# A graph layer with routed experts: 125-row transfers cut into 112 and 13 rows, and a rebuilt expert stage

## The chip, the cores and the metric

The kernel runs on one core of one Trainium2 chip. The core has five engines that run beside one another, each with its own instruction queue: PE (TensorE, matrix products), DVE (VectorE), ACT (ScalarE), POOL (GpSimd) and SP (SyncE, which here only issues transfers). Transfers between the chip's memory and the on-chip buffers run on 16 DMA engines. The metric is device time in microseconds (us) of one launch; less is better.

## The reference

The input is 1250 nodes of 768 values, and 41,250 directed edges. One layer is computed:

```python
xn = layernorm(x)
x  = x + gnn(xn, edges) + mix(xn)        # gnn: two graph-attention layers, 4 heads of 512, then 1 of 768
x  = x + ffn(layernorm(x))               # mix: random-feature attention of 8 heads, linear in the nodes

# ffn: two-level routing, 2 of 4 groups and 2 of 8 experts in each, so 4 of 32 experts for a node
comb = combine_weights(xf)               # [1250, 32], four entries of a row are not zero
h = gelu(einsum('nd,edm->nem', xf, W1) + b1)     # W1 [32, 768, 384]
y = einsum('nem,emd->ned', h, W2) + b2           # W2 [32, 384, 768]
out = einsum('ne,ned->nd', comb, y)
```

## The kernel before

**Tiling.** The 1250 nodes are 10 tiles (NT) of 125 rows (P); rows lie on the partitions of the on-chip buffers. All arithmetic is float32 but for selection matrices in bfloat16. There is no scheduler: each stage writes one instruction list per engine by hand, with semaphores between them, and a barrier of all engines ends a stage.

**Stages.** In order of time: norm (layernorm of x, 0 to 60 us), mix in two halves (60 to 485), proj (its output product and the first residual x1, 485 to 615), count (edges are turned into a dense matrix of edge counts, 615 to 938), mask (counts turned, masks and row maxima, 938 to 1053), gat1 (first attention layer, head by head, 1053 to 1470), gat2p and gat2 (second layer, 1470 to 1903), route norm (1903 to 1968), route (logits to expert choices, 1968 to 2033), expert (2033 to 2648).

**Transfers.** SP issues almost all of them, in program order, and waits in its queue hold back what is behind. Where a tensor is cut into tiles of 125 rows its transfer has 125 rows on the chip's side too: the loads of x in two halves (L131), x for the residual (L314), the count rows of a mask tile (L907), the 50 loads of a count tile for attention (L1048), x1 and the masks together (L1260, L1261), and the stores of x1, of the normed rows and of the output. Vectors needed on all rows are spread over 125 partitions by `partition_broadcast(P)`.

**Route.** POOL makes constants, DVE picks the experts, PE counts and ranks the nodes of each expert. DVE then makes `posm` (rank of a node within each expert, -1 where it isn't chosen), `ntile` (turns of 128 nodes per expert) and `tstart` (first turn of each).

**Expert stage.** Work goes by turns: one turn is up to 128 nodes of one expert, and there are 52 turns here. For each turn DVE compares rank minus offset with a row of 0 to 127 (Q, L1928), PE multiplies Q with `codes` (10 short products, PI, L1995) and thereby finds which nodes they are and their gates; DVE makes indices of them (L1887 to L1895), POOL gathers the rows (X) by an indirect transfer, PE turns X (TX, L2006), DVE and ACT copy it to xT, PE multiplies it with W1 (PH, 6 products of 384 columns with xT held still, L2034), DVE adds the bias, ACT takes gelu, PE turns h (TH, L2013), ACT copies hT, PE multiplies with W2 (PY, L2023), DVE and ACT scale by the gate into y, and POOL adds y into the output by an indirect transfer (L1850). It is a pipeline over four turns: while turn n is looked up, n-1 is in the first product and n-2 in the second. Four experts' weights are held at a time (NB = 4); SP loads the next ones as slots come free, and issues the first four at the end of the route norm's list. A stage's closing barrier stands in the trace under the line of the stage's `with ExitStack()`: L1456 for route norm, L1590 for route.

## Time and profile before

| | |
|---|---|
| median of 3 runs | 2640.47 us (2627.52 to 2644.08) |
| profiled execution, span | 2648.0 us (its own device time is not given beside it; the span is 7.5 us over the median) |
| PE busy | 2149.9 us, 81% |
| DVE busy | 1172.5 us, 44% |
| ACT busy | 443.9 us, 17% |
| POOL busy | 190.2 us, 7% |
| hardware transfer queue q1 | 82727 packets, 210.86 MB |
| mean transfer rate | 105 GB/s |

The span is the time from the first to the last instruction of the profiled execution. "Busy" is the time in which an engine had an instruction under way, so what is missing to the span is waiting. An average over 11 stages with different limits says little; the rows further down are taken stage by stage. "PEclk" is the clock granted to PE as a share of 2.4 GHz: 1.0 is full speed and 0.5 is 1.2 GHz. "DMA share" is how much of the 16 DMA engines' time was taken.

### The profile page before, as it was taken

To read this page: it belongs to the slowest core of one execution; us is meant where nothing else is said; L and a number is where in the kernel's file an instruction comes from. 1 tells how busy PE (TensorE), PEld (TensorE's weight loads), DVE (VectorE), ACT (ScalarE), POOL (GpSimd) and SP (SyncE) were. 2 spreads that over 40 slices of the span, in tenths; PEclk is the share of its full clock that TensorE was granted. 3 is DMA by queue.
4 is the path that set the end of the run, shared out by engine and by line. 5 is a ranking of instruction groups with operands and counts; after the bars stand their busy time and mean duration, and the time that the engine had idled before them with its cause. 6 is when DMAs were issued, how large, how long until landed. Compare 5 with 4: busy or idle time off the path is not lost. (4 is left out here: it accounts for less than half of the span.)

```text
span 2648.0 us, 32969 instructions
## 1 busy us (share of the span) xinstructions
PE 2149.9 (81%) x8696; PEld 1415.3 (53%) x8697; DVE 1172.5 (44%) x2660; ACT 443.9 (17%) x721; POOL 190.2 (7%) x205
## 2 busy tenths in 40 slices
PE   2998998596999922599999799539846888988997
PEld 1666665452555512488888455215543555555554
DVE  3113213133666626579888011056434444444442
ACT  1232112100111112122222000000000222222221
POOL 0000000000000000000000000000001222222222
PEclk9998998897999955799999899769956999989999
DMA  4001200113000045222322411321152777778653
GB/s 162 40 0 63 81 0 36 70 44 117 23 23 24 22 150 184 112 111 95 115 99 81 161 62 55 130 80 48 31 206 81 207 210 225 219 240 257 163 122 66
DMA packets 104535, 278.90 MB, mean 105 GB/s; under 512 B 8053, under 2 KB 53159, under 8 KB 103067
## 3 DMA queue, kind: packets, MB, share of 16 engines
q1 hardware_dynamic: 82727, 210.86, 22.6%
q0 software_dynamic: 15184, 55.37, 9.1%
q10 hardware_dynamic: 6560, 11.86, 1.2%
q8 instruction: 37, 0.61, 0.1%
q14 instruction: 27, 0.21, 0.0%
HBM read 214.49 MB, written 63.57 MB: 105 GB/s over the span
## 5 line engine op out<-in xcount | busy, mean ns | idle before, releaser
L1179 PE MATMUL gat_Z<-h,gat_wt 125*125 125x256 f32 (+1 forms) x1600 | 356.4, 382 | 40.0 <-DVE gat_wt L1095 40.0
L1179 PEld LDWEIGHTS gat_Z<-h,gat_wt 125*125 125x125 f32 x1600 | 299.3, 189 | 85.7 <-DVE gat_wt L1095 40.5
L2034 PE MATMUL ex_PH<-ex_w,ex_xT 128*128 x636 | 240.3, 532 | 24.2 <-DVE ex_xT L1883 14.5
L542 PE MATMUL mix_G<-mix_w,mix_xs 128*125 128x384 f32 x720 | 243.4, 489 | 0.0
L2023 PE MATMUL ex_PY<-ex_w,ex_hT 128*128 (+1 forms) x660 | 223.7, 489 | 15.9 <-POOL ex_hT L1838 14.8
L825 PE MATMUL count_G<-gnn_w,xnT 128*125 (+1 forms) x480 | 214.3, 596 | 18.5 <-issue 18.5
L1329 PE MATMUL gat2p_Y<-gat2p_w,gat2p_hT 128*125 128x384 f32 x640 | 209.3, 491 | 12.2 <-DMA gat2p_w<-in_L_gnn_W 12.2
L2034 PEld LDWEIGHTS ex_PH<-ex_w,ex_xT 128*128 128x128 f32 x636 | 126.9, 207 | 109.7 <-issue 48.2
L2023 PEld LDWEIGHTS ex_PY<-ex_w,ex_hT 128*128 128x128 f32 x660 | 126.1, 191 | 105.0 <-issue 18.8
L542 PEld LDWEIGHTS mix_G<-mix_w,mix_xs 128*125 128x125 f32 x720 | 133.4, 189 | 85.1 <-issue 2.6
L1329 PEld LDWEIGHTS gat2p_Y<-gat2p_w,gat2p_hT 128*125 128x125 f32 x640 | 121.3, 190 | 99.8 <-issue 14.9
L825 PEld LDWEIGHTS count_G<-gnn_w,xnT 128*125 128x125 f32 x480 | 88.4, 189 | 118.1 <-issue 116.6
L1441 PE MATMUL gat_Z<-h,gat_wt 125*125 125x385 f32 (+1 forms) x400 | 131.5, 491 | 15.7 <-DVE gat_wt L1399 15.7
L804 DVE SCALAR_TENSOR_TENSOR count_A<-count_ikey,count_off,keyT 128x512 f32 x120 | 90.2, 752 | 99.7 <-issue 68.3
L1910 DVE TENSOR_TENSOR ex_h<-ex_PH,ex_b 128x384 f32<-128x384 f32 x53 | 29.6, 558 | 205.8 <-PE ex_PH L2034 205.8
L1850 POOL DMA_INDIRECT out_rows<-ex_y,ex_idS x56 | 88.2, 1574 | 413.6 <-DVE ex_y L1905 295.4
L495 DVE TENSOR_REDUCE mix_nrm<-mix_sq 125x4 f32<-125x384 f32 x40 | 22.1, 553 | 215.5 <-ACT mix_sq L515 215.5
L1441 PEld LDWEIGHTS gat_Z<-h,gat_wt 125*125 125x125 f32 x400 | 75.6, 189 | 71.4 <-DVE gat_wt L1399 16.2
L810 DVE TENSOR_SCALAR count_B<-count_islo,sloT 128x314 f16 x480 | 112.1, 299 | 0.0
L347 PE MATMUL proj_Y<-proj_w,proj_aT 128*125 128x384 f32 x240 | 81.5, 498 | 26.4 <-DVE proj_x L387 26.4
L1275 DVE COPY h<-gat2p_Y 125x384 f32<-125x384 f32 x10 | 5.6, 559 | 194.8 <-PE gat2p_Y L1329 194.8
L1928 DVE TENSOR_TENSOR ex_Q<-ex_rel,ex_iota 125x1280 bf16<-125x1280 f32 x52 | 77.6, 1492 | 28.9 <-DVE ex_rel L1921 28.8
(292 smaller groups left out, 2456.9 us busy)
## 6 DMA issues: line engine op xcount, KB each, us to landing
ex_w<-in_L_ffn_W SPq DMA_DIRECT2D x64, 1152.0 KB, 8.0
gat_cnt<-c_dram SPq DMA_DIRECT2D x50, 610.4 KB
...
```

Source lines behind the costliest of these rows:

```text
L347: last = pe.matmul(Y[j][:], aT[b][:, k, :], w[:, k, j * 384:(j + 1) * 384], start=(k == 0), stop=(k == KD - 1))
L542: last = pe.matmul(G[c][:], xs[b][:, k, :], w[:, k, c, :], start=(k == 0), stop=(k == KD - 1))
L804: dve.scalar_tensor_tensor(A[:, bass.ds(s * RB, RB), :], ikey[:].unsqueeze(1).to_broadcast([128, RB, 128]), off[:, bass.ds(hd * NT + t, 1) ...
L810: last = dve.tensor_scalar(B[:, bass.ds(s * RB + b, 1), :], islo[:].unsqueeze(1), sloT[:, bass.ds(r * RB + b, 1)], None, ALU.is_equal)
L825: last = pe.matmul(G[t % 2][:], xnT[:, k, t * P:(t + 1) * P], w[:, k, bass.ds(hd * C1, C1)], start=(k == 0), stop=(k == KD - 1))
L1179: last = pe.matmul(Z[b][j][:], wt[b][:, s, :], h[:, s, bass.ds(hd, 1), j * HC:(j + 1) * HC + j], start=(s == 0), stop=(s == NT - 1))
L1329: last = pe.matmul(Y[b][j][:], hT[b][:, k, :], w[:, k, j * HW:(j + 1) * HW], start=(k == 0), stop=(k == KF - 1))
L1441: last = pe.matmul(Z[b][j][:], wt[b][:, s, :], h2[:, s, 385 * j:385 * j + CW[j]], start=(s == 0), stop=(s == NT - 1))
L1850: pool.indirect_dma_start(out, bass.IndirectOffsetOnAxis(ap=idS[:, 0:1], axis=0), y[:], None, compute_op=ALU.add).then_inc(added, 16)
L1928: dve.tensor_tensor(Q[:], rel[:].unsqueeze(2).to_broadcast([P, NT, SLOT]), iot[:].unsqueeze(1).to_broadcast([P, NT, SLOT]), ALU.is_equal). ...
L2023: last = pe.matmul(PY[j][:], hT[:, k, :], w2[:, bass.ds(b, 1), k, j * 384:(j + 1) * 384], start=(k == 0), stop=(k == KM - 1))
L2034: last = pe.matmul(PH[:], xT[:, k, :], w1[:, bass.ds(b, 1), k, :], start=(k == 0), stop=(k == KD - 1))
```

## The change

**Transfers.** A new constant PM = 112. Every transfer of 125 rows becomes two, of rows 0 to 111 and 112 to 124, on the same queue, with the waits counting both (`rows_dma` and two loops). Tiles that receive a vector on all partitions have 128 rows instead of 125, and the spread goes to all 128.

**Route.** A table of turns is made: `etab` (expert of each turn), `offs` (128 times the turn's number within its expert) and `total` (number of turns). PE makes sums with ones and triangular matrices in one new buffer TB (16 short products), DVE rounds up to tiles and compares, and nine steps on a 1-row tile fall away. Two copies into `codes` go from DVE to POOL.

**Expert stage.** The host lays W1, W2 and b1 out anew, so that a partition's share of an expert's weights is one contiguous piece (128x2304 instead of 128x6x384 and 128x3x768); b1 is loaded once, turned. The first product is turned: W1 is held still and xT moves, 18 products of 128 columns into three buffers, whose result is h already turned; ACT adds the bias inside gelu and writes hT. The TH turn, the DVE bias addition and the copy of hT fall away. Q is made from `posm`, `offs` and the table in one instruction (`find`). Indices and gates are kept in four slots. Loops run over the turns of the table, and the order within a turn is new on every engine.

```diff
 SLOPE = 0.2
+PM = 112
...
+def rows_dma(eng, dst, src, sem):
+    eng.dma_start(dst[0:PM], src[0:PM]).then_inc(sem, 16)
+    eng.dma_start(dst[PM:P], src[PM:P]).then_inc(sem, 16)
...
-                sp.dma_start(xa[:, h * HT:(h + 1) * HT, :], x.rearrange("(t p) d -> p t d", p=P)
-                             [:, h * HT:(h + 1) * HT, :]).then_inc(x_loaded[h], 16)
+                rows_dma(sp, xa[:, h * HT:(h + 1) * HT, :],
+                         x.rearrange("(t p) d -> p t d", p=P)[:, h * HT:(h + 1) * HT, :], x_loaded[h])
...
-                sp.dma_start(ct[b][:], ct_dram.rearrange("(d a) s -> d (a s)", a=SPLIT)[t * P:(t + 1) * P, 0:N]
-                             ).then_inc(loads[b], 16)
+                rows_dma(sp, ct[b], ct_dram.rearrange("(d a) s -> d (a s)", a=SPLIT)[t * P:(t + 1) * P, 0:N], loads[b])
...
-                    sp.dma_start(cnt[t % 2][:], c_dram[t, :, :].rearrange("p (t d) -> p t d", d=P)
-                                 ).then_inc(c_loaded[t % 2], 16)
+                    rows_dma(sp, cnt[t % 2], c_dram[t, :, :].rearrange("p (t d) -> p t d", d=P), c_loaded[t % 2])
...
-            sp.dma_start(x1[:], x1_dram.rearrange("(t p) d -> p t d", p=P)).then_inc(x_loaded, 16)
-            sp.dma_start(mask[:], mask_dram.rearrange("t p n -> p t n")).then_inc(mask_loaded, 16)
+            rows_dma(sp, x1, x1_dram.rearrange("(t p) d -> p t d", p=P), x_loaded)
+            rows_dma(sp, mask, mask_dram.rearrange("t p n -> p t n"), mask_loaded)
             sp.wait_ge(copied, 3)
             sp.dma_start(al2T_dram, alT[:]).then_inc(stored, 16)
             sp.wait_ge(stored, 16)
-            sp.dma_start(row[:], al2T_dram[0, :].partition_broadcast(P)).then_inc(row_loaded, 16)
-            sp.dma_start(rows_t[:], al2T_dram[1, :].partition_broadcast(P)).then_inc(rows_loaded, 16)
+            sp.dma_start(row[:], al2T_dram[0, :].partition_broadcast(128)).then_inc(row_loaded, 16)
...
                     sp.wait_ge(xn_ready, i * 2 + (b + 1))
-                    sp.dma_start(xn2_dram[bass.ds(i * (2 * P) + b * P, P), :], xn[b][:]).then_inc(stored[b], 16)
+                    for lo, n in ((0, PM), (PM, P - PM)):
+                        sp.dma_start(xn2_dram[bass.ds(i * (2 * P) + (b * P + lo), n), :], xn[b][lo:lo + n, :]
...
                 sp.wait_ge(summed, 2 * t + 2)
-                sp.dma_start(out[t * P:(t + 1) * P, :], x1[:, t, :]).then_inc(stored, 16)
-            sp.wait_ge(stored, 16 * (NT + 1))
+                for lo, n in ((0, PM), (PM, P - PM)):
+                    sp.dma_start(out[t * P + lo:t * P + lo + n, :], x1[lo:lo + n, t, :]).then_inc(stored, 16)
...
+            dve.wait_ge(tab_pe, 1)
+            step(dve.tensor_scalar(tiles_i[:], TB[0:NE, 0:1], float(SLOT - 1), None, ALU.add))
+            step(dve.tensor_scalar(tiles_i[:], tiles_i[:], SLOT.bit_length() - 1, None, ALU.logical_shift_right))
+            step(dve.tensor_copy(tiles[:], tiles_i[:]))
+            step(dve.tensor_scalar(tiles[:], tiles[:], 1.0, None, ALU.max))
+            dve.tensor_copy(tiles_w[:], tiles[:].to_broadcast([NE, P])).then_inc(tiles_ready, 1)
...
+            dve.wait_ge(tab_pe, 2)
+            step(dve.tensor_copy(ends[:], TB[0:NE, 8:9]))
+            dve.tensor_scalar(past[:], turn[0:NE, 0, :], ends[:], None, ALU.is_ge).then_inc(ends_ready, 1)
+            dve.tensor_copy(tstart[:], TB[0:1, 16:16 + NE])
+            dve.tensor_copy(ntile[:], TB[0:1, 72:72 + NE])
+            dve.tensor_copy(total[:], TB[0:1, 64:65]).then_inc(turns_ready, 1)
...
+            dve.wait_ge(tab_pe, 3)
+            dve.tensor_copy(etab[:], TB[0:1, 128:128 + NTAB])
+            dve.scalar_tensor_tensor(offs[:], TB[0:P, 256:256 + NTAB], -float(SLOT), turn[:, 1, :], ALU.mult, ALU.add)
...
+            for t in range(NT):
+                last = pe.matmul(TB[0:NE, 0:1], sele[:, t * NG:(t + 1) * NG, :].rearrange("p a e -> p (a e)"),
+                                 ones[:, 0:1], start=(t == 0), stop=(t == NT - 1))
+            last.then_inc(tab_pe, 1)
...
+            pe.wait_ge(tiles_ready, 1)
+            pe.matmul(TB[0:NE, 8:9], tri[:, 0, :], tiles[:], start=True, stop=True)
+            pe.matmul(TB[0:1, 16:16 + NE], tiles[:], tri[:, 1, :], start=True, stop=True)
+            pe.matmul(TB[0:1, 72:72 + NE], tiles[:], ident[0:NE, 0:NE], start=True, stop=True)
+            pe.matmul(TB[0:1, 64:65], tiles[:], ones[0:NE, 0:1], start=True, stop=True).then_inc(tab_pe, 1)
+            pe.wait_ge(ends_ready, 1)
+            pe.wait_ge(turns_ready, 1)
+            pe.matmul(TB[0:1, 128:128 + NTAB], ones[0:NE - 1, 0:1], past[0:NE - 1, :], start=True, stop=True)
+            pe.matmul(TB[0:P, 256:256 + NTAB], tiles_w[0:NE - 1, :], past[0:NE - 1, :], start=True, stop=True
+                      ).then_inc(tab_pe, 1)
...
+def load_expert(eng, W1, W2, weights, w_loaded, e, b):
+    w1, w2 = weights
+    eng.dma_start(w1[:, b, :, :], W1[e, :, :, :].rearrange("o p k n -> p (o k) n")).then_inc(w_loaded[b], 16)
+    eng.dma_start(w2[:, b, :, :], W2[e, :, :, :].rearrange("o p k n -> p (o k) n")).then_inc(w_loaded[b], 16)
...
+                    done = sp.value_load(tstart[0:1, bass.ds(i * NB + (b + 1 - NB), 1)], min_val=1, max_val=MAXT)
+                    sp.wait_ge(gemm2, done)
+                    load_expert(sp, W1, W2, weights, w_loaded, bass.ds(i * NB + b, 1), b)
...
+            def gather(n):
+                pool.wait_ge(idx_ready, n + 1)
+                if not (isinstance(n, int) and n == 0):
+                    pool.wait_ge(x_turned, n)
+                    pool.wait_ge(gathered, n * 16)
+                pool.sem_inc(passed, 1)
                 pool.indirect_dma_start(X[:], None, xn2_dram, bass.IndirectOffsetOnAxis(ap=idG[:, 0:1], axis=0)
                                         ).then_inc(gathered, 16)
...
             def scatter(n):
...
+                pool.wait_ge(y_d, n + 1)
+                pool.wait_ge(y_a, n + 2)
+                pool.wait_ge(idS_ready, n + 1)
+                pool.sem_inc(passed, 1)
                 pool.indirect_dma_start(out, bass.IndirectOffsetOnAxis(ap=idS[:, 0:1], axis=0), y[:], None,
...
+            with pool.Fori(0, end) as i:
+                gather(i + 2)
+                scatter(i)
...
+            def find(n):
+                e = expert_of(dve, n)
+                at = n if isinstance(n, int) else dve.snap(n)
+                if not (isinstance(n, int) and n == 0):
+                    dve.wait_ge(ids_done, n)
+                dve.scalar_tensor_tensor(Q[:], posm[:, :, bass.ds(e, 1)].to_broadcast([P, NT, SLOT]),
+                                         offs[:, bass.ds(at, 1)],
+                                         iot[:].unsqueeze(1).to_broadcast([P, NT, SLOT]),
+                                         ALU.subtract, ALU.is_equal).then_inc(q_ready, 1)
+            def indices(n):
+                slot = slot_of(dve, n)
+                dve.wait_ge(ids_done, n + 1)
+                dve.wait_ge(y_a, n)
+                dve.tensor_copy(cod[:], PI[:]).then_inc(ids_copied, 1)
+                dve.wait_ge(ids_copied, n + 1)
+                dve.scalar_tensor_tensor(gate[:, slot], cod[:, 5:6], cod[:, 4:5], cod[:, 3:4], ALU.add, ALU.add)
+                dve.scalar_tensor_tensor(idf[:, 0:1], cod[:, 1:2], float(P), cod[:, 0:1], ALU.mult, ALU.add)
+                dve.scalar_tensor_tensor(idf[:, 1:2], cod[:, 2:3], -1.0, pad[:], ALU.add, ALU.mult
+                                         ).then_inc(found, 1)
+                dve.wait_ge(found, n + 1)
+                dve.tensor_tensor(ids[:, slot], idf[:, 0:1], idf[:, 1:2], ALU.subtract).then_inc(ids_ready, 1)
+                dve.wait_ge(ids_ready, n + 1)
+                if not (isinstance(n, int) and n == 0):
+                    dve.wait_ge(gathered, n * 16)
+                dve.tensor_scalar(idG[:], ids[:, slot], 1.0, None, ALU.mult).then_inc(idx_ready, 1)
             def turn_x(n):
...
+                dve.wait_ge(x_half, n + 1)
                 dve.tensor_copy(xT[:, 0:3, :], TX[0][:]).then_inc(xT_d, 1)
...
+            def second(n):
+                slot = slot_of(dve, n)
                 dve.wait_ge(added, n * 16)
...
+                dve.tensor_scalar(idS[:], ids[:, slot], 1.0, None, ALU.mult).then_inc(idS_ready, 1)
+                dve.wait_ge(gemm2, n + 1)
+                dve.tensor_scalar(y[:, 0:384], PY[0][:], gate[:, slot], None, ALU.mult).then_inc(y_d, 1)
+            dve.wait_ge(consts, 2)
+            find(0)
+            end = turns(dve)
+            indices(0)
+            find(1)
+            indices(1)
+            find(2)
+            turn_x(0)
+            with dve.Fori(0, end) as i:
+                indices(i + 2)
+                find(i + 3)
+                turn_x(i + 1)
+                second(i)
...
+            def first(n):
+                e = expert_of(act, n)
+                act.wait_ge(gemm2, n)
+                for m in range(KM):
+                    act.wait_ge(gemm1, n * KM + (m + 1))
+                    act.activation(hT[:, m, :], PH[m][:], ACT.Gelu, bias=b1T[:, bass.ds(act.snap(e * KM + m), 1)]
+                                   ).then_inc(h_gelu, 1)
...
+                slot = slot_of(act, n)
+                act.wait_ge(idx_ready, n + 1)
+                act.wait_ge(added, n * 16)
+                act.wait_ge(gemm2, n + 1)
+                act.activation(y[:, 384:768], PY[1][:], ACT.Copy, scale=gate[:, slot]).then_inc(y_a, 1)
...
+            with act.Fori(0, end) as i:
+                first(i)
+                turn_x(i + 1)
+                second(i)
...
+            def find(n):
+                e = expert_of(pe, n)
+                pe.wait_ge(q_ready, n + 1)
+                if not (isinstance(n, int) and n == 0):
+                    pe.wait_ge(ids_copied, n)
...
+            def first(n, b):
+                pe.wait_ge(xT_d, n + 1)
+                pe.wait_ge(xT_a, n + 1)
+                for m in range(KM):
+                    pe.wait_ge(h_gelu, n * KM + (m + 1))
+                    for k in range(KD):
+                        last = pe.matmul(PH[m][:], w1[:, b, k, m * 128:(m + 1) * 128], xT[:, k, :],
+                                         start=(k == 0), stop=(k == KD - 1))
+                    last.then_inc(gemm1, 1)
...
+                pe.wait_ge(y_d, n)
+                pe.wait_ge(y_a, n + 1)
+                pe.wait_ge(h_gelu, n * KM + 2 * KM)
...
                     for k in range(KM):
-                        last = pe.matmul(PY[j][:], hT[:, k, :], w2[:, bass.ds(b, 1), k, j * 384:(j + 1) * 384],
+                        last = pe.matmul(PY[j][:], hT[:, k, :], w2[:, b, k, j * 384:(j + 1) * 384],
...
+            with pe.register("ex_turn_pe") as turn:
+                pe.reg_mov(turn, 0)
+                with pe.Fori(0, NE // NB) as i:
+                    for b in range(NB):
+                        pe.wait_ge(w_loaded[b], i * 32 + 32)
+                        count = pe.value_load(ntile[0:1, bass.ds(i * NB + b, 1)], min_val=1, max_val=NT)
+                        with pe.Fori(0, count) as _:
+                            n = pe.snap(turn)
+                            find(n + 2)
+                            first(n, b)
+                            turn_x(n + 1)
+                            second(n, b)
+                            pe.reg_add(turn, turn, 1)
...
+    o["L0_ffn_W1"] = np.asarray(i["L0_ffn_W1"]).reshape(NE, KD, 128, FM).transpose(0, 2, 1, 3)
+    o["L0_ffn_W2"] = np.asarray(i["L0_ffn_W2"]).reshape(NE, KM, 128, D).transpose(0, 2, 1, 3)
+    o["L0_ffn_b1"] = np.asarray(i["L0_ffn_b1"]).reshape(NE * KM, 128).T
```

Where the change writes the code in another order, the engines' own instruction orders show it. First DVE in the expert loop, before (`leaving`, `waiting` and `found` pass the indices of earlier turns on):

```order
L1928 TENSOR_TENSOR ex_Q<-ex_rel,ex_iota 125x1280
L1898 REGISTER_ALU
L1899 CAST ex_idS<-ex_leaving 128x1
L1900 COPY ex_gS<-ex_leaving 128x1
L1903 COPY ex_leaving<-ex_waiting 128x2
L1877 ISA
L1905 TENSOR_SCALAR ex_y<-ex_PY,ex_gS 128x384
L1883 COPY ex_xT<-ex_TX 128x384
L1934 TENSOR_SCALAR ex_rel<-ex_rel 125x10
L1877 REGISTER_ALU
L1886 REGISTER_ALU
L1887 COPY ex_cod<-ex_PI 128x6
```

and in the changed kernel, behind the copy to `cod` and the gate, which wait for `y_a` (`etab` is the table of experts, and TENSOR_LOAD reads it into a register):

```order
L1906 SCALAR_TENSOR_TENSOR ex_idf<-ex_cod 128x1
L1907 SCALAR_TENSOR_TENSOR ex_idf<-ex_cod,ex_pad 128x1
L1910 REGISTER_ALU
L1910 TENSOR_TENSOR ex_ids<-ex_idf 128x1
L1913 REGISTER_ALU
L1914 TENSOR_SCALAR ex_idG<-ex_ids 128x1
L1838 ISA
L1838 TENSOR_LOAD etab
L1838 ISA x2
L1894 ISA
L1894 SCALAR_TENSOR_TENSOR ex_Q<-posm,offs,ex_iota 125x1280
L1918 COPY ex_xT<-ex_TX 128x384
```

Q stood first in the turn, with the copy to xT behind it and the index steps last; now the index steps stand first, and Q and the copy to xT come behind them.

Then PE in the expert loop of the changed kernel, behind the ten PI products:

```order
L2001 ISA
L2003 MATMUL ex_PH<-ex_xT,ex_w 128x128 x6
L2001 REGISTER_ALU
L2003 MATMUL ex_PH<-ex_xT,ex_w 128x128 x6
L2001 REGISTER_ALU
L2003 MATMUL ex_PH<-ex_xT,ex_w 128x128 x6
L1987 ISA
L1994 MATMUL ex_TX<-ident,ex_X 128x128 x6
L2010 REGISTER_ALU
L2013 MATMUL ex_PY<-ex_w,ex_hT 128x384 x6
```

Before, the order was TX, TH, PI, PH, PY; now PI is first, PH is 18 products of 128 columns, TX stands between PH and PY, and there is no TH.

Last SP at the end of the route norm's list, before:

```order
L1482 DMA xn_dram<-rn_xn 125x768
L1479 REGISTER_ALU
L1479 COMPARE_AND_BRANCH
L1751 DMA ex_w<-in_L_ffn_W 128x6x384
L1758 DMA ex_b<-in_L_ffn_b 128x384
L1759 DMA ex_w<-in_L_ffn_W 128x3x768
```

and now:

```order
L1490 DMA xn_dram<-rn_xn 112x768
L1490 ISA
L1490 DMA xn_dram<-rn_xn 13x768
L1486 REGISTER_ALU
L1486 COMPARE_AND_BRANCH
L2133 DMA ex_b1T<-in_L_ffn_b 128x96
L1796 DMA ex_w<-in_L_ffn_W 128x2304
L1797 DMA ex_w<-in_L_ffn_W 128x2304
```

The store of 125 rows became two, and the three transfers of an expert, of which four experts are issued here, became two with contiguous pieces in memory.

## Rows read from the trace of the kernel before

**Rows 1.** The page: its head, and its row on the expert stage's comparison
```profile
span 2648.0 us, 32969 instructions
...
L1928 DVE TENSOR_TENSOR ex_Q<-ex_rel,ex_iota 125x1280 bf16<-125x1280 f32 x52 | 77.6, 1492 | 28.9 <-DVE ex_rel L1921 28.8
```

**Rows 2.** View by windows: window, PE, PEld, DVE, ACT, POOL busy, PEclk, DMA share, GB/s
```profile
1474.00:1488.00 14.00, 9.72 (x22) 5.52 (x23) 0.00 (x0) 0.00 (x0) 0.00 (x0) 0.66 1.03 405
1700.00:1720.00 20.00, 0.00 (x0) 0.00 (x0) 0.00 (x0) 0.00 (x0) 0.00 (x0) 0.50 0.32 130
938.00:1053.00 115.00, 26.87 (x110) 22.88 (x110) 62.86 (x95) 26.77 (x40) 10.93 (x21) 0.50 0.54 185
2045.00:2636.00 591.00, 525.87 (x2265) 328.10 (x2265) 252.09 (x817) 137.88 (x240) 137.31 (x107) 0.95 0.70 192
```

**Rows 3.** The waits: engine, line, awaited: total us, times, longest us
```profile
DVE stats L153 <- DMA xa<-in_x: 31.7, 2, 18.4
...
DVE proj_x L382 <- DMA proj_x<-in_x: 28.8, 1, 28.8
...
DVE mask_ct L937 <- DMA mask_ct<-ct_dram: 58.1, 9, 27.3
...
DVE gat_u L1083 <- DMA gat_rows<-mT_dram: 23.2, 1, 23.2
...
DVE gat2p_junk L1297 <- DMA gat2p_row<-al2T_dram: 43.8, 1, 43.8
...
DVE rn_xn L1508 <- DMA xn_dram<-rn_xn: 19.3, 8, 4.1
...
DVE rt_gl L1648 <- PEq L1456: 17.0, 1, 17.0
```

**Rows 4.** The waits of the transfer queue SP, same columns
```profile
SPq L1590 <- DMA out_rows<-x: 10.7, 1, 10.7
```

**Rows 5.** Timeline, mask stage: start, duration, engine, line, operation, [idle before]
```profile
945.64 0.29 DVE L937 TENSOR_TENSOR mask_ct<-mask_ct,ident 125x125 f32<-125x125 f32 x1 [18.77 <-DMA mask_ct<-ct_dram]
```

**Rows 6.** Timeline of one turn of the expert stage, undisturbed
```profile
2597.61 0.82 PE L2006 MATMUL ex_TX<-ident,ex_X 128*128 128x128 f32 x6
...
2597.81 0.58 ACT L1959 ACTIVATE ex_y<-ex_PY,ex_gS 128x384 f32<-128x384 f32 x1 [2.35 <-PE ex_PY L2023]
...
2598.59 0.40 PE L1995 MATMUL ex_PI<-codes,ex_Q 125*128 x10
...
2599.29 0.17 DVE L1887 COPY ex_cod<-ex_PI 128x6 f32<-128x6 f32 x1
...
2599.52 4.13 PE L2034 MATMUL ex_PH<-ex_w,ex_xT 128*128 x12 [0.53 <-DVE ex_xT L1883]
...
2600.56 0.15 DVE L1895 CAST ex_idG<-ex_found 128x1 int32<-128x1 f32 x1
...
2601.61 1.01 POOL L1842 DMA_INDIRECT ex_X<-xn_dram,ex_idG  x1 [0.55 <-issue]
...
2603.49 4.03 PE L2023 MATMUL ex_PY<-ex_w,ex_hT 128*128 x12
...
2607.36 0.82 PE L2006 MATMUL ex_TX<-ident,ex_X 128*128 128x128 f32 x6
```

**Rows 7.** The chain that ended last, expert stage: start, duration, what
```profile
2231.63 8.58 DMA ex_X<-xn_dram,ex_idG
...
2242.35 7.03 PE ex_PH L2034 x12
...
2635.99 1.55 POOL out_rows L1850
```

**Rows 8.** Timeline of the mix stage, PE: short matmuls behind 128-column loads
```profile
89.01 1.92 PE L570 MATMUL mix_KV<-mix_vs,mix_phik 125*128 125x97 f32 x16
```

**Rows 9.** Timeline of SP, end of the route norm: the last expert transfer is issued
```profile
1966.59 0.94 SPq L1759 DMA_DIRECT2D ex_w<-in_L_ffn_W  x1
```

**Rows 10.** Timeline, first instruction of the expert stage
```profile
2033.73 0.24 POOL L1829 IOTA ex_iota<- 125x128 f32 x1 [59.80 <-POOLq L1590]
```

More of the change, by code:

```diff
@@ L1010, in gat1_phase @@
     with ExitStack() as st:
[L1011 to L1012 removed]
+        brow = sb(nc, st, "gat1_brow", [128, F1])
+        rows = [sb(nc, st, f"gat1_rows{b}", [128, 2, N]) for b in range(2)]
         u = sb(nc, st, "gat1_u", [P, NT, P])
@@ L1861, in _ @@
-            gather()
-            scatter(None)
-            with pool.register("ex_turn_pool") as turn:
-                end = turns(pool, turn, body)
-                for k in range(3):
-                    scatter(end + k)
-                pool.wait_ge(added, (end + 3) * 16)
+            gather(0)
+            gather(1)
+            end = turns(pool)
+            with pool.Fori(0, end) as i:
+                gather(i + 2)
+                scatter(i)
+            pool.wait_ge(gathered, end * 16 + 32)
@@ L2038, in _ @@
[L2038 to L2067 removed]
+            find(0)
```

405 lines of the change are left out of this document (125 added, 280 removed).

## Prediction

> **What bounds the kernel now.** I read the page first, for the head [rows 1]. Then I took the view by windows, stage by stage [rows 2]. It shows two kinds of stretch. In the expert stage PE is busy 525.87 of 591 us at 0.95 of its clock, so PE sets the pace there. In others PE does nothing: from 1700 to 1720 nothing runs but a transfer, that of x1 and the masks, 125 rows each. It moves 130 GB/s and takes 0.32 of the DMA engines' time, which is 5 of 16. From 1474 to 1488 a transfer of 128 rows runs at 405 GB/s and a share of 1.03. So 125-row transfers run at a third of the rate. Third came the waits, for where that rate is waited for [rows 3, 4]. Fourth the timeline of one turn of the expert stage [rows 6] and its chain [rows 7]. The chain there runs mostly through PE, with a gather in it now and then. One turn takes 2607.36 - 2597.61 = 9.75 us when undisturbed; the stage, from 2033.73 [rows 10] to 2648.0, is 614.3 us for 52 turns [rows 1], so some 11.2 on average with start and end: gathers of up to 8.58 and PH at 7.03 where it takes 4.13 else [rows 7] are the rest.
>
> **The sum, first half: transfers.** I take 400 GB/s for the 112 and 13 rows together, where 130 stand now.
> - x at the start: two halves of 1.92 MB, 14.7 us each at 130 and 4.8 at 400. DVE waits 31.7 [rows 3]. It gets back about 20 by rate, and up to 3 more where the second half is no longer waited for: 23.
> - x in proj: 28.8 waited [rows 3], 3.84 MB behind two spread vectors. It saves 25.
> - count rows of the mask stage: 58.1 in 9 waits [rows 3]. The big one comes at the second tile (18.77, [rows 5]), behind four spread rows of 0.62 MB each. I take 22 there. Behind it DVE becomes the limit: it is busy 62.86 us in the 115 us of the stage [rows 2], 6.3 a tile, so of the rest only about 11 go. Sum 33.
> - start of gat1: brow, four spread rows and the first count tile are 4.15 MB, 31.7 us now and 10.5 then; the wait is 23.2 [rows 3], and 20 of it go.
> - gat2p: 3.84 MB of x1 and 6.25 of masks stand ahead of a small store and the spread row that DVE waits 43.8 us for [rows 3]. They shrink from 77 to 25 us, which lie beside the products of the last tiles; about 6 remain. It saves 38.
> - stores of the normed rows: 19.3 waited in 8 waits [rows 3]; PE and DVE then take turns, so only 4 go.
> - barrier behind the route norm: DVE waits 17.0 [rows 3] until SP has issued twelve transfers of weights and bias, the last at 1966.59 [rows 9]. Now there are nine with contiguous pieces, and the three-part stores of bias to all rows are gone. If issuing is held back by the number of pieces, 16 go; if by bytes, the rate is that of before and nothing goes. I take 16 and keep 0.
> - last store of the route stage: 10.7 [rows 4], 3 then, saves 7.
> - gat2's start and the 50 count loads: nothing counted. They lie beside PE's products, but for some 5 us that I leave out.
> - route table: 16 products, of which the two groups behind `tiles` are waited for, and eight DVE steps instead of nine. No row shows them; by the steps of 0.15 to 0.17 [rows 6] the new chain costs 1 to 6 us. I take 3.
>
> Together 23 + 25 + 33 + 20 + 38 + 4 + 16 + 7 - 3 = **163 us** saved, between 130 and 185.
>
> A rule of the Trainium skill speaks against the halving (DMA: Bandwidth & Descriptors, Rules for kernel authors): two transfers to disjoint partition halves "serialize", and one is to be used. By it the first half of the sum would be near zero, but for the nine transfers of the barrier. The trace can't decide it for 112 rows; it only shows that 125 and 128 rows differ threefold [rows 2]. The same page (Why a DMA increments its semaphore by 16 and not by 1) has the number of engines as the largest divisor up to 16 of the slowest dimension. By it 125 rows take 5, 112 take 16 and 13 take 13, and the sum as above stands.
>
> **The sum, second half: a turn of the expert stage.** PE's own work in a turn: PI .4, PH, TX .7, PY 3.9 [rows 6]. PH is now 36 short products (two passes each); 16 products of 97 columns behind loads of 128 took 1.92 us [rows 8], 0.12 each, so 4.3 instead of 4.13. TH (.4) falls away. So PE would want 9.3 a turn instead of 9.75, and little was to be had.
>
> But the order on DVE makes a ring. In turn i the index steps of turn i+2 come first, and they wait until `y_a` is i+2. It starts at 1 and ACT adds one for each finished y. So it is i+2 only when ACT has done y of turn i, and that is behind PE's second product of turn i. Behind the index steps on DVE stand the table read, Q of turn i+3 and the copy to xT of turn i+1; PE's next instruction is PI of i+3, which needs Q, and then PH of i+1, which needs xT. So nothing of the next turn begins on PE before this chain has run:
> - ACT y: .58 [rows 6] and .2 to notice, .8
> - index steps: from cod at 2599.29 to the end of idG at 2600.71 [rows 6] there are seven steps in 1.42 us; now six, two of them not waited for, 1.0
> - table read into a register: no row. Between the .55 that POOL spends in its loop instructions and the 1.01 of issuing a gather [rows 6]; .8
> - Q: 1.49 [rows 1]
> - PI: .40 where its sequencer ran ahead [rows 6]; here ten pairs of a register step and a product start behind the wait. Between .4 and 1.5; 1.2
> - hand-overs: .3 from the end of PI to cod [rows 6]
>
> That is 5.6 us in which PE stands or does PI, against none now. Meanwhile the xT copies (.55) are hidden behind PI. Then PH 4.3, TX .65, PY 3.87: **14.4 us a turn**.
>
> The gather: its indices are ready 1.8 us behind the second product, TX comes at 5.6 + 4.3 = 9.9, so 8.1 are free for 1.01 of issue and up to 8.58 of transfer [rows 6, 7]. It is mostly covered, and becomes late only in the worst cases. The scatter is issued behind it and has a whole turn. Weights: SP loads an expert 3 experts ahead, of 2.36 MB, 6 us at 400 GB/s; a longer turn gives more time.
>
> The clock: PE now has a gap of 4 to 5 us in every turn. Where such gaps stand today, PH takes up to 7.03 instead of 4.13 [rows 7], 2.9 more; in other stages with PE busy 26.87 of 115 us the clock is 0.50 [rows 2]. I take 1.8 a turn, between 1 and 3. So 16.2 us.
>
> Start and end: 11 us until TX of turn 0 (Q 1.49, PI, indices, gather 1.01 and some 5), and behind the last product 5.6 of the same ring, 1 for a gather that nobody needs, 1.55 for the scatter, and from there to the end as today, 2648.0 - 2637.5 = 10.5 [rows 7]. Together 30. The stage is 30 + 52 × 16.2 = 872 us against 614.3: **258 us** lost.
>
> The whole: 2648.0 - 163 + 258 = 2743 as a span. The span of the profiled execution is 7.5 us over the median of the runs shown, so against those 2743 - 7.5, about 2735 us, 3.6% slower. A measurement of this kernel tells about 1% from no change, here 26 us.
>
> **The rivals.**
> - *Forecast*, chance 0.63: the ring with the clock falling in the gaps. Bounds: turns of 15.4 to 17.6 (-42 to +73) and savings of 130 to 185 (+33 to -22), so 2670 to 2815.
> - *The ring with the clock held*, 0.17: 14.4 a turn, or PI at .4 and the table read hidden and the clock a bit lower. The stage is 779, 165 lost, 2648 - 163 + 165 - 7.5 = 2642: no change. For it speaks that PE is still busy 9 of 14.4 us, and that the whole expert stage is at 0.95 today with gaps in it [rows 2]; against it the PH of 7.03.
> - *No ring*, 0.08, the faster side. If the wait for `y_a` is satisfied in time, since I have misread which turn's y it needs, DVE runs ahead of PE as today and PE sets the pace: 30 + 52 × 9.3 = 514, 100 saved, and 2648 - 163 - 100 - 7.5 = 2378. It decides once the index steps of i+2 can run before y of turn i is done. Against it: the count of `y_a` by the code. For it: four slots are there, which would be enough for two turns more.
> - *The split brings nothing*, 0.07: the two parts take the DMA engines of one, 13 rows slower than their share, so only the barrier's 16 are saved; 2648 - 16 + 3 + 258 - 7.5 = 2886. Against it stands the 0.32 [rows 2], with 11 engines idle. The rule of the Trainium skill on disjoint halves, named above, would have it so.
> - Something else, 0.05, above all a clock at half speed throughout (PE's 8.8 doubled, some 23 us a turn, past 3000).
>
> **How the numbers follow.** The likeliest gives 2735. Range: 2610 to 2820, from the lower bound of the clock-held case (2642 less 22 and a little) to the upper end of the forecast; it leaves out the no-ring case, the split that brings nothing and the rest, 0.20. Faster by over 1% (below 2614): the no-ring case 0.08, and 0.05 of the clock-held case with all savings: 0.13. Within 1% (2614 to 2667): 0.12 of the clock-held case and 0.03 of the forecast: 0.15. Slower: 0.72.
>
> **What would show it.** Windows like those of 1700 to 1720 at a share near 1 and some 400 GB/s, waits for x, mask rows and the spread row of gat2p below 10 us each. In the expert stage PE's idle time should stand ahead of PI with Q as releaser, 52 times 4 to 5 us, and Q should start some 2.6 us behind ACT's y, each turn; the granted clock of the stage below 0.9. Wrong it would be if Q lay beside PH or PY, or if TX were released by the gather in most turns (then the gather, not the ring, is the limit), or if the split transfers still took a third of the DMA engines.

## The result: 2791.8 us after 2640.2, slower, inside the range

The changed kernel takes 2791.78 us (median of 4 runs, 2789.44 to 2792.03), the kernel before 2640.17 (2627.52 to 2644.08): a ratio of 1.057, 95% interval 1.054 to 1.060. The forecast was 2735 us, range 2610 to 2820.

The page of the changed kernel, its head and three rows of the expert stage, to be read beside [rows 1]:

```profile
span 2790.1 us, 33764 instructions
...
L2003 PE MATMUL ex_PH<-ex_xT,ex_w 128*128 128x128 f32 x1872 | 328.9, 358 | 7.3 <-issue 1.8
...
L1982 PE MATMUL ex_PI<-codes,ex_Q 125*128 x540 | 72.3, 185 | 245.6 <-DVE ex_Q L1894 245.6
L1903 DVE COPY ex_cod<-ex_PI 128x6 f32<-128x6 f32 x54 | 8.9, 165 | 651.9 <-ACT ex_y L1960 648.9
```

The first product (PH) holds 328.9 us against 240.3 before, and PE stands 245.6 us ahead of PI, waiting for Q (54 look-ups of 10 products). The index steps (`cod`) wait 648.9 us for ACT's y.

Where the time went, by the first instruction of each stage in the two traces:

| stage | before, us | after, us | difference |
|---|---|---|---|
| norm | 57.3 | 41.5 | -15.8 |
| mix | 433.3 | 430.7 | -2.6 |
| proj | 122.7 | 105.9 | -16.8 |
| count | 324.3 | 323.0 | -1.3 |
| mask and gat1 | 531.0 | 473.5 | -57.5 |
| gat2p | 287.1 | 253.8 | -33.3 |
| gat2 | 147.6 | 143.7 | -3.9 |
| route norm | 63.9 | 43.3 | -20.6 |
| route | 65.7 | 57.8 | -7.9 |
| all ahead of the expert stage | 2032.9 | 1873.2 | -159.7 |
| expert | 614.3 | 916.1 | +301.8 |

The waits after, to be read beside [rows 3]; SP waits 1.9 us where [rows 4] has 10.7:

```profile
DVE mask_ct L946 <- DMA mask_ct<-ct_dram: 27.6, 2, 16.0
...
DVE proj_x L392 <- DMA proj_x<-in_x: 16.8, 1, 16.8
DVE stats L162 <- DMA xa<-in_x: 15.9, 2, 11.8
...
DVE gat_u L1091 <- DMA gat_rows<-mT_dram: 12.0, 1, 12.0
...
DVE gat2p_junk L1305 <- DMA gat2p_row<-al2T_dram: 10.4, 1, 10.4
...
DVE rn_xn L1517 <- DMA xn_dram<-rn_xn: 1.1, 1, 1.1
...
DVE rt_gl L1675 <- PEq L1463: 0.3, 1, 0.3
```

They are down to between .06 and .58 of before, and the barrier's 17.0 to 0.3. One turn of the expert stage, to be read beside [rows 6]:

```profile
2590.62 6.30 PE L2003 MATMUL ex_PH<-ex_xT,ex_w 128*128 128x128 f32 x36
...
2596.75 0.82 PE L1994 MATMUL ex_TX<-ident,ex_X 128*128 128x128 f32 x6
...
2597.47 4.14 PE L2013 MATMUL ex_PY<-ex_w,ex_hT 128*128 128x384 f32 x12
...
2601.87 0.58 ACT L1960 ACTIVATE ex_y<-ex_PY,ex_gate 128x384 f32<-128x384 f32 x1 [3.77 <-PE ex_PY L2013]
...
2602.48 0.17 DVE L1903 COPY ex_cod<-ex_PI 128x6 f32<-128x6 f32 x1 [12.43 <-ACT ex_y L1960]
...
2604.52 1.55 DVE L1894 SCALAR_TENSOR_TENSOR ex_Q<-posm,offs,ex_iota 125x1280 bf16<-125x1280 f32 x1 [0.72 <-issue]
...
2606.22 1.32 PE L1982 MATMUL ex_PI<-codes,ex_Q 125*128 x10 [4.62 <-DVE ex_Q L1894]
...
2607.68 1.65 PE L2003 MATMUL ex_PH<-ex_xT,ex_w 128*128 128x128 f32 x6
```

From one PH (2590.62) to the next (2607.68) pass 17.06 us, where one turn took 9.75. The granted clock of the stage is 0.80 (1886 to 2780), where [rows 2] has 0.95. It reads as forecast: y, index steps, 0.72 of nothing before Q ("issue": the table read), Q, PI, and only then PH. The end of PY at 2601.61 lies 6.07 us ahead of the next PH.

### The profile page after: what moved, and what is told of

Read it like the earlier page. It is cut to its first block and busy times, and to the rows that moved or that the text cites. A ratio compares the mean times of both kernels' runs of the same rounds, so it can differ in the third digit from the quotient of the medians.

```text
span 2790.1 us, 33764 instructions
## 1 busy us (share of the span) xinstructions
PE 2262.0 (81%) x9786; PEld 1605.9 (58%) x9787; DVE 1104.1 (40%) x2372; ACT 418.7 (15%) x743; POOL 245.4 (9%) x197
## 5 line engine op out<-in xcount | busy, mean ns | idle before, releaser
L1187 PE MATMUL gat_Z<-h,gat_wt 125*125 125x256 f32 (+1 forms) x1600 | 354.7, 381 | 20.5 <-DVE gat_wt L1103 20.5
L2003 PE MATMUL ex_PH<-ex_xT,ex_w 128*128 128x128 f32 x1872 | 328.9, 358 | 7.3 <-issue 1.8
L2003 PEld LDWEIGHTS ex_PH<-ex_xT,ex_w 128*128 128x128 f32 x1872 | 319.2, 271 | 11.5 <-issue 11.5
L1982 PE MATMUL ex_PI<-codes,ex_Q 125*128 x540 | 72.3, 185 | 245.6 <-DVE ex_Q L1894 245.6
L1903 DVE COPY ex_cod<-ex_PI 128x6 f32<-128x6 f32 x54 | 8.9, 165 | 651.9 <-ACT ex_y L1960 648.9
L835 PE MATMUL count_G<-gnn_w,xnT 128*125 (+1 forms) x480 | 214.7, 597 | 17.6 <-issue 17.5
L1982 PEld LDWEIGHTS ex_PI<-codes,ex_Q 125*128 125x128 bf16 x540 | 56.3, 104 | 289.9 <-issue 278.3
L2013 PE MATMUL ex_PY<-ex_w,ex_hT 128*128 128x384 f32 x624 | 215.2, 495 | 0.0
L1867 POOL DMA_INDIRECT ex_X<-xn_dram,ex_idG x54 | 113.5, 2101 | 653.2 <-DVE ex_idG L1914 635.2
L2013 PEld LDWEIGHTS ex_PY<-ex_w,ex_hT 128*128 128x128 f32 x624 | 114.5, 190 | 75.9
L1952 ACT ACTIVATE ex_hT<-ex_PH,ex_b1T 128x128 f32<-128x128 f32 x156 | 57.3, 367 | 566.9 <-PE ex_PH L2003 566.9
```

What stands on the lines that cost most here:

```text
L835: last = pe.matmul(G[t % 2][:], xnT[:, k, t * P:(t + 1) * P], w[:, k, bass.ds(hd * C1, C1)], start=(k == 0), stop=(k == KD - 1))
L1187: last = pe.matmul(Z[b][j][:], wt[b][:, s, :], h[:, s, bass.ds(hd, 1), j * HC:(j + 1) * HC + j], start=(s == 0), stop=(s == NT - 1))
L1867: pool.indirect_dma_start(X[:], None, xn2_dram, bass.IndirectOffsetOnAxis(ap=idG[:, 0:1], axis=0)).then_inc(gathered, 16)
L1982: last = pe.matmul(PI[:], Q[:, t, :], codes[:, t, bass.ds(e, 1), :].rearrange("p o c -> p (o c)"), start=(t == 0), stop=(t == NT - 1))
L2003: last = pe.matmul(PH[m][:], w1[:, b, k, m * 128:(m + 1) * 128], xT[:, k, :], start=(k == 0), stop=(k == KD - 1))
L2013: last = pe.matmul(PY[j][:], hT[:, k, :], w2[:, b, k, j * 384:(j + 1) * 384], start=(k == 0), stop=(k == KM - 1))
```

## The experiments

Each interval is that of the ratio to the kernel before, run beside it. "Stage" is the expert stage of the profiled execution.

| kernel | us | against before, interval | stage, us |
|---|---|---|---|
| changed | 2791.8 | 1.054 to 1.060 | 916.1 |
| e1_loose | 2383.4 | 0.899 to 0.905 | 518.9 |
| e2_fill | 2746.1 | 1.038 to 1.045 | 877.9 |
| e3_pm115 | 2895.1 | 1.094 to 1.100 | 914.4 |
| e4_split_only | 2497.2 | 0.942 to 0.948 | 616.3 |
| e5_fill18 | 2746.2 | 1.038 to 1.046 | 877.7 |
| e6_q_first | 2614.8 | 0.988 to 0.995 | 743.5 |
| e7_pm80 | 2802.1 | 1.060 to 1.068 | 913.6 |
| e8_loose_old_weights | 2393.3 | 0.904 to 0.910 | 518.6 |
| e9_fill_between | 2769.9 | 1.046 to 1.054 | 900.8 |
| e10_loose_pm120 | 2418.8 | 0.913 to 0.918 | 519.1 |

### The ring: e1_loose

```diff
                 dve.wait_ge(ids_done, n + 1)
-                dve.wait_ge(y_a, n)
+                dve.wait_ge(y_a, 1 if isinstance(n, int) else n - 1)
                 dve.tensor_copy(cod[:], PI[:]).then_inc(ids_copied, 1)
```

> The changed kernel, but the index steps of turn i+2 wait for ACT's y of turn i-1 instead of that of turn i (the four slots allow it). Ring theory (the wait for y_a, with what stands behind it on DVE, holds PE up once a turn and lets its clock fall): the 4.6 us of idle PE ahead of PI go from every turn, PH falls from 6.30 to about 4.3 and the turn from 17.06 to between 9.5 and 10.5 us; 2791.8 - 52 x 6.9 = about 2430 us. Rival, gather theory (with the ring gone each turn waits for the rows of its own gather, 2.1 us of issue and 5 to 8 of transfer, ahead of TX): turns of 11.5 to 13, 2500 to 2580 us. Rival, the turned product is slow by itself (36 short products at 0.175 each whatever the gaps): PH stays near 6.3, turns of 11.5 with no idle PE.

Measured 2383.4 us: 408 less than the changed kernel, for one number, and 9.8% less than before. A turn late in the stage:

```profile
2300.60 0.58 ACT L1960 ACTIVATE ex_y<-ex_PY,ex_gate 128x384 f32<-128x384 f32 x1 [5.98 <-DMA out_rows<-ex_y,ex_idS]
...
2301.29 0.15 DVE L1903 COPY ex_cod<-ex_PI 128x6 f32<-128x6 f32 x1
...
2302.32 0.82 PE L1994 MATMUL ex_TX<-ident,ex_X 128*128 128x128 f32 x6
...
2303.04 4.14 PE L2013 MATMUL ex_PY<-ex_w,ex_hT 128*128 128x384 f32 x12
...
2303.43 1.55 DVE L1894 SCALAR_TENSOR_TENSOR ex_Q<-posm,offs,ex_iota 125x1280 bf16<-125x1280 f32 x1 [0.71 <-issue]
...
2307.02 0.40 PE L1982 MATMUL ex_PI<-codes,ex_Q 125*128 x10
...
2307.27 4.26 PE L2003 MATMUL ex_PH<-ex_xT,ex_w 128*128 128x128 f32 x36
...
2311.37 0.82 PE L1994 MATMUL ex_TX<-ident,ex_X 128*128 128x128 f32 x6
```

TX follows TX after 9.05 us. Q lies beside PY (2303.43 to 2304.98), PI takes 0.40 as in [rows 6], PH 4.26. PE's two largest waits within the stage:

```profile
PE ex_PI L1982 <- DVE ex_Q L1894: 10.9, 3, 6.5
PE ex_TX L1994 <- DMA ex_X<-xn_dram,ex_idG: 7.4, 5, 2.5
```

With two more of 1.2 us, 19.5 us in all of 518.9. The ring is shown, and both rivals fall: TX waits for a gather 5 times, 7.4 us, and the turned product is as fast as the old one. The gain was larger than expected since turns came at 9.4 on average ((518.9 - 30) / 52) and not 10.2.

### The ring's items: e6_q_first

```diff
-                indices(i + 2)
                 find(i + 3)
+                indices(i + 2)
                 turn_x(i + 1)
```

> The changed kernel with the wait for y_a kept, but DVE does the table read and Q of turn i+3 ahead of the index steps of turn i+2 that hold this wait. By the ring's items, .72 and 1.55 leave the chain and PI runs beside the index steps: from the end of PY to the start of PH 3.1 us instead of 6.07, turns of 14.1 at the clock of now and 12.2 if it stays up, so 2792 - 52 x 3 to 52 x 4.9, 2540 to 2640 us. Rival: the gather, which then has only about 5 us between its indices and TX, becomes late in most turns (waits of TX for DMA ex_X): turns of 14 to 15, 2640 to 2690 us.

Measured 2614.8 us, inside the first forecast. The wait stands as it was, and only what stood behind it is less:

```profile
2400.34 0.82 PE L1994 MATMUL ex_TX<-ident,ex_X 128*128 128x128 f32 x6
...
2401.06 4.14 PE L2013 MATMUL ex_PY<-ex_w,ex_hT 128*128 128x384 f32 x12
...
2406.07 0.17 DVE L1903 COPY ex_cod<-ex_PI 128x6 f32<-128x6 f32 x1 [8.99 <-ACT ex_y L1960]
...
2406.50 1.34 PE L1982 MATMUL ex_PI<-codes,ex_Q 125*128 x10 [1.30 <-DVE ex_cod L1903]
...
2407.99 5.91 PE L2003 MATMUL ex_PH<-ex_xT,ex_w 128*128 128x128 f32 x36 [0.15 <-DVE ex_xT L1918]
...
2414.40 0.76 PE L1994 MATMUL ex_TX<-ident,ex_X 128*128 128x128 f32 x5 [0.50 <-DMA ex_X<-xn_dram,ex_idG]
```

PE waits 1.30 us ahead of PI instead of 4.6; PY's end to PH is 2.8 us (2405.20 to 2407.99), where 3.1 were worked out; this turn is 14.06, and from one TX to the next it is 13.7 on average. TX waits for the gather here, but only 0.50 us. Over the stage the rival is there in part:

```profile
PE ex_TX L1994 <- DMA ex_X<-xn_dram,ex_idG: 32.9, 28, 2.8
```

In 28 turns the gather is late, 32.9 us in all, where the changed kernel waits for it once (2.5 us). So the price is a sum along the ring, and what stands on it can be taken off, but then the next wait begins to show. PH stays at 5.91 in most turns although the gap is a third: the clock needed its own tests.

### The clock: e2_fill, e5_fill18, e9_fill_between

e2 and e5 (with 18 for 12):

```diff
                             n = pe.snap(turn)
+                            for _f in range(12):
+                                pe.matmul(PH[0][:], ident[:], ident[:], start=True, stop=True)
                             find(n + 2)
```

> The changed kernel with its ring untouched, but PE multiplies the identity with itself 12 times (24 passes) at the head of each turn, in the gap in which it would stand; the results go nowhere. If the falling clock costs PE time behind the gap: the passes take about 2.8 us of the 4.6, PH falls from 6.30 to 4.3 to 4.6, the turn from 17.06 to about 15, and the kernel gains 90 to 120 us (2670 to 2700) although it does more work. If PH is slow by itself, nothing is gained (2792), or some us are lost if the passes run over the gap.

> The changed kernel with its ring untouched and 18 products of the identity (36 passes) at the head of each turn instead of 12, so that PE's gap of 4.6 us ahead of PI is all but closed; their results go nowhere. With 12 the clock was 1.0 through the gap and then fell to 0.5 for some 3 us inside PH (5.91 instead of 6.30). If it is PE's pause that makes it fall, it now stays up: PH 4.1 to 4.4, turn about 15.0, some 85 us less than with 12, about 2660 us. If the ten thin PI products alone (1.3 us with little work in them) are pause enough, PH stays at 5 to 5.9 and the gain over 12 is below 40 us.

Measured 2746.1 and 2746.2. Of e2's 46 us, 38 are in the stage, less than half of what was expected; and e5 adds nothing though PE's wait ahead of PI is down to 0.58 us. The expectation that PE's pause alone brings the clock down is wrong. The view by windows of e5, one turn of the frequent kind, columns as in [rows 2] (PE busy first, PEclk after the five engines):

```profile
2499.90:2500.90 1.00, 0.86 (x8) 0.72 (x8) 0.00 (x0) 0.00 (x0) 0.15 (x1) 1.00 1.02 433
2500.90:2501.90 1.00, 1.00 (x8) 1.00 (x7) 0.00 (x0) 0.00 (x0) 1.00 (x1) 0.60 0.94 393
2501.90:2502.90 1.00, 1.00 (x7) 1.00 (x6) 0.00 (x0) 0.00 (x0) 0.43 (x1) 0.50 0.71 295
2502.90:2503.90 1.00, 1.00 (x7) 1.00 (x7) 0.00 (x0) 0.37 (x1) 0.00 (x0) 0.50 1.23 98
2503.90:2504.90 1.00, 1.00 (x8) 1.00 (x8) 0.00 (x0) 0.00 (x0) 0.00 (x0) 0.69 0.92 163
2504.90:2505.90 1.00, 1.00 (x11) 1.00 (x11) 0.00 (x0) 0.37 (x1) 0.00 (x0) 1.00 0.70 132
```

From 2500.90 on PE is busy all the time, and yet the clock is at 0.50 (1.2 GHz) for some 3 us, behind PI's ten products of 6 columns, which take 1.33 us: the trace has a register step ahead of each, 0.12 us apart. But not every turn is like that. Two turns in a row, with the same pause and the same PI:

```profile
2156.81 1.33 PE L1982 MATMUL ex_PI<-codes,ex_Q 125*128 x10 [0.58 <-DVE ex_Q L1894]
2158.28 4.28 PE L2003 MATMUL ex_PH<-ex_xT,ex_w 128*128 128x128 f32 x36
...
2173.32 5.91 PE L2003 MATMUL ex_PH<-ex_xT,ex_w 128*128 128x128 f32 x36
```

In e5 13 of the 52 first products take about 4.3 us, in e2 and in e6 12, and in the changed kernel none. What parts the two kinds of turn is not shown. e9 puts a dense product behind each of the first nine of them, on top of e5:

```diff
                                      start=(t == 0), stop=(t == NT - 1))
+                    if t < NT - 1:
+                        pe.matmul(PH[0][:], ident[:], ident[:], start=True, stop=True)
```

> The kernel of e5_fill18, with one product of the identity behind each of the first nine PI products too, so that the stretch of PI (1.33 us for ten products of 6 columns, paced by register steps) is dense. PI then takes about 2.4 us, 1.0 more on the ring. If this thin stretch is what brings the clock down, it now stays up, PH falls from 5.91 to 4.1 and the turn gains 0.8: 2746 - 40 = about 2705 us. If the clock falls all the same, 55 us are lost: 2800 us, and what brings it down stays open.

```profile
2499.00:2500.00 1.00, 0.56 (x5) 0.55 (x6) 1.00 (x4) 0.00 (x0) 1.00 (x1) 1.00 0.00 0
...
2502.00:2503.00 1.00, 1.00 (x10) 0.98 (x10) 0.00 (x0) 0.00 (x0) 0.82 (x1) 1.00 0.23 92
2503.00:2504.00 1.00, 1.00 (x11) 1.00 (x10) 0.00 (x0) 0.00 (x0) 0.00 (x0) 1.00 0.90 68
2504.00:2505.00 1.00, 1.00 (x11) 1.00 (x10) 0.00 (x0) 0.37 (x1) 0.00 (x0) 1.00 0.84 120
```

The clock stays at 1.00 through the same stretch, and PH takes 4.26 in place of 5.91, here and in all 52 turns:

```profile
2502.49 4.26 PE L2005 MATMUL ex_PH<-ex_xT,ex_w 128*128 128x128 f32 x36
...
2516.05 0.18 PE L1982 MATMUL ex_PI<-codes,ex_Q 125*128 x1 [0.59 <-DVE ex_Q L1894]
```

So the clock's part is shown, and with a pause of 0.6 us it is the thin PI behind it that decides: filled (and at 3.05 us for 1.47 longer), PH is never slowed; thin, it is in 39 turns of 52. The time was missed: 2769.9 and not 2705, 24 us slower than e5. The pairs in the stretch of PI come every 0.335 us, 3.05 us in all (2499.44 to 2502.49) and not 2.4. Against the turns of e5 in which the clock fell this eats what PH gave back (16.61 us a turn and 16.67); against the 13 in which it had not fallen (15.05) it is a loss of 1.6 each, 20 of the 23 us by which the stage is longer. In e1 nothing of it arises: PI's steps run ahead during PY.

### The transfers: e4_split_only, e3_pm115, e7_pm80, e10_loose_pm120

e4 is the kernel before with the transfers alone changed: the rows cut at 112, and the vectors spread to 128 rows.

> The kernel before, with only the transfers changed (112 and 13 rows, vectors spread to 128 rows); route and expert stage and the layout of the weights as before. By the stages of the two traces the parts ahead of the route stage are 152 us shorter after the change, of which 17 are the barrier that waited for the expert weights to be issued; the route's last store gives 4 to 7. Expected 2640 - 140 = 2500 us (2485 to 2520), with the barrier's 17 us still there if it comes from the many pieces of the old weights' layout or from the bias spread to all rows. If transfers at the higher rate collide with others or are given back later, less is gained.

Measured 2497.2 us, 142 less than the 2639.5 of the kernel before beside it, and the stage took 616.3 us as before (614.3). Nothing is given back later, and DVE's barrier wait is still 12.3 us. Then only one number of the changed kernel:

```diff
-PM = 112
+PM = 115
```

> The changed kernel with PM = 115 instead of 112: the transfers go as 115 and 10 rows, two pieces as before. If the gain comes from how many DMA engines a transfer of so many rows is spread over (115 = 23 x 5 gives 5, like 125, where 112 gives 16), the row transfers fall back to about 130 GB/s and 60 to 110 us are lost, most of it in the norm, proj and gat2p stages (16, 15 and 33 us), while the vectors spread to 128 rows keep their gain; 2850 to 2900 us. If two pieces in place of one bring the gain whatever their size, the time stays at 2792.

Measured 2895.1 us, 103 lost. Its view by windows, and that of the changed kernel, of the first load of x:

```profile
2.00:16.00 14.00, 0.00 (x0) 0.00 (x0) 0.00 (x0) 0.09 (x1) 0.00 (x0) 1.00 0.34 125
```
```profile
2.00:16.00 14.00, 0.00 (x0) 0.00 (x0) 4.04 (x9) 0.08 (x1) 0.00 (x0) 1.00 1.01 243
```

A share of 0.34 and 125 GB/s against 1.01 and 243. Two pieces alone bring nothing here; it is the number of rows that spreads a transfer over the engines. By the Trainium skill (DMA: Bandwidth & Descriptors, Why a DMA increments its semaphore by 16 and not by 1) 115 rows go on 5 engines and 112 on 16, and the shares agree. Its advice against two transfers to disjoint partition halves ("they serialize", Rules for kernel authors) is not borne out here, where the whole transfer took a share of 0.32; no run halves one that has all the engines.

e3 also parts what e4 gained. It is 104 us longer than the changed kernel ahead of the expert stage, but still 55 shorter than the kernel before: 20 of these in the route norm, where the weights' layout counts, and 34 in mask and gat1, where e3 too spreads vectors to 128 rows. So of e4's 142 us about 104 come from the rows cut at 112, and most of the rest, by what is left over, from the spread to 128; no run has that spread alone.

But 243 GB/s at a full share is not the 405 that 128 rows have at theirs [rows 2]. For this two more sizes:

```diff
-PM = 112
+PM = 80
```

> The changed kernel with PM = 80: pieces of 80 and 45 rows, for which the engines by the divisor rule are 16 and 15, with 5 + 3 rows on the busiest where 112 and 13 give 7 + 1. Expected the same as with 112, 2792 within 10 us. If it were the size of the large piece that counts (80 rows being further from 125 than 112 and 115), it would be other.

```diff
-PM = 112
+PM = 120
```

> The kernel of e1_loose (2383 us) with PM = 120: pieces of 120 and 5 rows. By the divisor rule 15 and 5 engines, 8 rows on a busy one. With 112 and 13 rows all engines are taken (share 1.01) and yet only 243 GB/s move at the start, with 80 and 45 rows 198, with 128 rows some 400. If what holds the rate down is that an engine's rows (7 and 1, or 5 and 3) are cut across the groups of 8 rows that an engine has in a transfer of 128, then 120 rows in eights go at about 350, the waits for x fall from 16 to 11 us and from 17 to 12, that of gat2p from 10 to below 3, and 15 to 30 us are gained: 2355 to 2370 us. If the number of engines alone counts, one engine fewer costs a little, and the time is 2383 to 2390 us.

Measured 2802.1 (10 slower, expected the same within 10) and 2418.8 (35 slower than e1, expected 15 to 30 faster). e7's true loss is larger: up to the route norm it is 19 us behind the changed kernel, and its route norm ran at the higher clock, 31.9 us for 43.3, which the last section comes back to. At the start:

```profile
2.00:16.00 14.00, 0.00 (x0) 0.00 (x0) 2.20 (x5) 0.08 (x1) 0.00 (x0) 1.00 1.00 198
```
```profile
2.00:16.00 14.00, 0.00 (x0) 0.00 (x0) 0.72 (x2) 0.08 (x1) 0.00 (x0) 1.00 0.98 187
```

198 and 187 GB/s at a full share. The theory of groups of 8 rows fell, and counting engines alone does not give it either. The packets of these stretches are all but a few of 3072 bytes, and it is they that take longer: 0.18 us each (median) with 112 and 13 rows, 0.23 with 80 and 45, 0.24 with 120 and 5, and 0.12 with 125 rows as with 128 [rows 2]. So the share counts time in which a packet is under way, and the same packet can take twice as long. Why it does stays open; 112 and 13 is the best of the four splits tried.

### The weights' layout: e8_loose_old_weights

On top of e1, W1 and W2 stay in the inputs' own order (W2 as W1):

```diff
-    eng.dma_start(w1[:, b, :, :], W1[e, :, :, :].rearrange("o p k n -> p (o k) n")).then_inc(w_loaded[b], 16)
+    eng.dma_start(w1[:, b, :, :], W1[e, :, :].rearrange("o (k p) n -> p (o k) n", p=128)).then_inc(w_loaded[b], 16)
...
-    o["L0_ffn_W1"] = np.asarray(i["L0_ffn_W1"]).reshape(NE, KD, 128, FM).transpose(0, 2, 1, 3)
```

> The kernel of e1_loose with W1 and W2 laid out as before (pieces of 1536 and 3072 bytes instead of 9216), b1 still loaded once. If the many pieces of the weights filled the queue at the end of the route norm, DVE's wait at the barrier comes back, 8 to 12 us, and in the expert stage gathers are late more often: 2395 to 2420 us. If it was the bias spread to all rows (4 issues of 3 to 4 us each in e4), the barrier stays at 0 to 3 us and the time at 2383.

Measured 2393.3 us, 10 more than e1 and just below the expected 2395 to 2420. The intervals, 0.904 to 0.910 and 0.899 to 0.905, overlap, so the 10 us are hardly clear of noise; the wait is:

```profile
DVE rt_gl L1675 <- PEq L1463: 15.9, 1, 15.9
```

The barrier's wait is back at 15.9 us, more than the 8 to 12 expected, with the bias still loaded once, so it is the many pieces. e1 has 0.3; but its route norm ran at the lower clock, and at the higher one, as here, e2 and e5 have 3.0 and 2.7, so 13 us is what the layout is worth at this barrier. In the expert stage it is worth nothing: 518.6 and 518.9 us, and gathers are late in 7 turns for 4.7 us, in e1 in 5 for 7.4.

## Why the prediction was right, and where it was off

**Transfers: 163 forecast, 159.7 measured**, and the total is better than its terms: that it is off by 3 only is luck, as terms that were too high and others too low cancel. I took 400 GB/s for the split transfers; they move 243 to 260, and the prediction's sign of waits below 10 us each for x, the mask rows and gat2p did not come (15.9 and 16.8, 27.6, 10.4). So x at the start gave 15.8 for 23, proj 16.8 for 25, gat2p 33.3 for 38. Mask and start of gat1 gave 57.5 for 53 (the first count tile, in the queue behind the spread rows, was late too: PE's wait for the first weights of gat1 fell from 40.0 to 20.5). gat2 gave 3.9 and mix 2.6, which I had left out (mix takes 425.9 to 433.0 us in the other traces, so its 2.6 need not come from the change), and route 7.9 for 4 (7 less the table's 3). Route norm gave 20.6 for 20, the barrier by pieces as taken. That the split works, against the rival's 0.07, is shown by e3 and e4. Of the 57.5 us in mask and gat1, e3 keeps 34 with its count rows cut at 115.

**The ring: right in mechanism and nearly in size.** Per turn, forecast and measured: y .8 and .87; index steps 1.0 and 1.32; table read .8 and .72; Q 1.49 and 1.55; PI 1.2 and 1.32; hand-overs .3 and .29. Together 5.6 and 6.07. Then PH 4.3 + 1.8 = 6.1 and 6.13 up to TX, TX .65 and .72, PY 3.87 and 4.14: 16.2 and 17.06. PY was taken where the next turn's TX overlapped it by .16; here nothing follows it, and it counts whole. Start and end were 30 and are 916.1 - 52 × 17.06 = 29. Two slips in the prediction changed nothing: 614.3 us over 52 turns are 11.8 with start and end and 11.2 without, and a clock term of at most 3 gives turns of up to 17.4, not 17.6.

**The clock's 1.8** came out at 2.0 (6.30 against e1's 4.26), but its reason, the gap alone, was incomplete: e5 shows that a pause of 0.58 us and the thin PI behind it are enough in 39 of 52 turns. The 1.8 was a choice between 1 and 3, so that it came so near is partly luck.

**The sum.** 2735 against 2791.8, 57 off: 44 from the expert stage (52 × 0.86, less 1 at start and end), 3 from the transfers, and 9 from the way from span to time. I took off 7.5 as the one profiled span lay over the median; the changed kernel's time is 1.8 over its span.

**The rivals.** "No ring" gave a stage of 514 and 2378 us; e1, which takes the ring away and nothing else, has 518.9 and 2383 (its profiled execution 2394.9). So PE's own turn was sized well, and what remained was whether the ring happens; that was to be had from counting the semaphore. "The split brings nothing" gave 2886 and e3 has 2895, but this is luck: e3 saves 55 us ahead of the expert stage where the rival had 13, loses 300 in that stage where it had 258, and 9 lie in the way from span to time.

**The best version** is e1_loose at 2383.4 us, 0.899 to 0.905 of before: 142 us from the transfers (e4), 97 from an expert stage in which PE waits 19.5 us in all (518.9 against 616.3), and most of the rest from the weights' layout at the barrier behind the route norm.
